# Issuing the store of the attention values from ScalarE, beside the copy that feeds it, instead of from SyncE

## The reference

```
xn  = layernorm(x)
q, k, v = xn Wq', xn Wk', xn Wv'              # 16 heads of 16
s   = softmax(causal(q k') / 4) v, heads joined, times Wo'
g   = silu( (silu(xn Wg'/127) * (xn Wu'/127)) Wd'/127 )
out = x + s * g
```

## Time and profile before

| | |
|---|---|
| median of 3 runs | 954.44 us (954.1 to 955.37) |
| the profiled execution's own time | 956.07 us |
| its span in the trace | 954.3 us |
| mean granted clock of TensorE | 0.995 of full speed |
| PE busy | 917.9 us, 96% |
| ACT busy | 584.3 us, 61% |
| POOL busy | 496.0 us, 52% |
| instructions | 22760 |

### The profile page before, as it was taken

One profiled execution on the slowest core, in us unless ns is written; L12 is line 12 of the kernel. 1 busy time (PEld: TensorE's weight loads), 2 busy tenths in 40 slices (PEclk: granted clock), 3 DMA queues, 4 the chain that ended last, 5 costly groups with the idle time before them and its releaser, 6 DMA issues.

```text
span 954.3 us, 22760 instructions
## 1 busy us (share of the span) xinstructions
PE 917.9 (96%) x9065; PEld 685.9 (72%) x9065; DVE 700.1 (73%) x950; ACT 584.3 (61%) x796; POOL 496.0 (52%) x681
## 2 busy tenths in 40 slices
PE   4999999999999999999999999999999999999994
PEld 3767767776868777686877768687686877768564
DVE  6985868787786977768687786868778686777823
ACT  5265675657576665757657575666657566575771
POOL 4253644737455473645547464474645547364552
PEclk9999999999999999999999999999999999999997
DMA  7704236344442535435353543534344353444323
GB/s 242 190 26 166 83 116 188 125 162 128 156 153 102 179 118 171 136 135 161 126 173 101 192 137 124 173 125 155 119 169 147 117 175 122 161 129 151 105 93 86
DMA packets 85468, 133.97 MB, mean 140 GB/s; under 512 B 13681, under 2 KB 35953, under 8 KB 85361
## 3 DMA queue, kind: packets, MB, share of 16 engines
q1 hardware_dynamic: 85360, 132.47, 42.0%
HBM read 53.22 MB, written 25.75 MB: 83 GB/s over the span
## 4 chain that ended last, share of the span: by engine, by line
PE 81%; issue 5%; POOL 4%; ACT 3%; DVE 3%; DMA 2%; SPq 0%; POOLq 0%; ACTq 0%; DVEq 0%
PE bank L194 44%; PE values L527 12%; PE bank L434 12%; PE bank L494 9%; PE bank L447 3%; POOL o_compact L568 2%; ACT probs L502 2%; DMA o_reciprocals<-scratch_r 1%; ACT o_hi L575 1%; DVE gated L379 1%; DVE row_max L457 1%; POOL probs L509 1%; PE bank L463 1%; PE bank L670 0%; DMA mean_and_rstd<-scratch_m 0%
## 5 line engine op out<-in xcount | busy, mean ns | idle before, releaser
L457 DVE TENSOR_REDUCE row_max<-bank 128x2 f32<-128x768 f32 (+3 forms) x352 | 384.8, 1124 | 61.6 <-PE bank L447 58.5
L502 ACT ACTIVATE probs<-bank 128x1024 f32<-128x1024 f32 x320 | 320.1, 1026 | 120.7 <-PE bank L494 119.3
L509 POOL TENSOR_SCALAR_AFFINE_SELECT probs<-probs 128x256 f32<-128x256 f32 (+1 forms) x448 | 194.2, 451 | 270.0 <-ACT probs L502 267.7
L527 PE MATMUL values<-probs,v 128*17 128x512 f32 (+3 forms) x2048 | 166.2, 436 | 4.9 <-POOL probs L509 4.8
L393 POOL TENSOR_TENSOR h_lo<-gated,h_hi 128x512 fp32r<-128x512 f32 x96 | 125.1, 1303 | 70.6 <-ACT h_hi L390 68.4
L434 PE MATMUL bank<-k_stack,q_stack 64*128 64x128 f32 (+3 forms) x1024 | 155.7, 364 | 2.7 <-DVE row_max L457 1.2
L494 PE MATMUL bank<-q_stack,k_stack 64*128 64x512 f32 (+3 forms) x1024 | 142.2, 350 | 1.3 <-DVE row_max L457 0.7
L434 PEld LDWEIGHTS bank<-k_stack,q_stack 64*128 64x128 f32 x1024 | 83.0, 185 | 69.7 <-issue 30.4
L494 PEld LDWEIGHTS bank<-q_stack,k_stack 64*128 64x128 f32 x1024 | 82.7, 185 | 39.2 <-issue 17.3
L366 DVE SCALAR_TENSOR_TENSOR gated<-gated,bank 128x512 f32<-128x512 f32 x96 | 65.8, 685 | 58.1 <-ACT gated L363 58.1
L194 PE MATMUL bank<-xt_hi,wg_hi 128*128 128x256 f32 x384 | 99.2, 292 | 2.3 <-DVE gated L379 2.3
(11 more groups left out here) (123 smaller groups left out, 1602.9 us busy)
## 6 DMA issues: line engine op xcount, KB each, us to landing
k_stack<-qk_hi SPq DMA_DIRECT2D x64, 256.0 KB, 2.5
q_stack<-qk_hi SPq DMA_DIRECT2D x64, 256.0 KB, 2.6
scratch_o<-o SPq DMA_DIRECT2D x64, 256.0 KB, 2.3
x_again<-x SPq DMA_DIRECT2D x16, 512.0 KB, 4.8
k_stack<-qk_lo SPq DMA_DIRECT2D x32, 256.0 KB, 2.5
q_stack<-qk_lo SPq DMA_DIRECT2D x32, 256.0 KB, 2.7
o_compact<-scratch_o SPq DMA_DIRECT2D x32, 256.0 KB
o_reciprocals<-scratch_r SPq DMA_DIRECT2D x32, 256.0 KB
```

What stands on the lines that cost most here:

```text
L457: signal(e.tensor_reduce(rows, scores, axis=AX.X, op=ALU.max), "d_sm")
L502: signal(e.activation(PR[:, (SCORES * beta + k) % SLOTS, :, :], both(banks), ACT.Exp, scale=SCALE_S), "d_ex")
L509: last = e.affine_select(out=diag, in_=diag, compare_op=ALU.is_ge, fill=0.0, base=0, pattern=[[0, many], [1, P]], channel_multiplier=-1)
L527: last = nc.tensor.matmul(PVB[32 * c:32 * c + VW, j * P:S], V[par][:, j, 4 * g + c, :], PR[:, (SCORES * beta + 5 * g + kind) % SLOTS, pari ...
```

## The change

SP's part of a third `pv` unit goes to ACT. The two waits (for the older readers of the scratch, `s_oc`, and for the copy, `d_ov`) and the DMA are the same, but they now stand in ACT's queue, right behind ACT's own copy.

```diff
             elif en == "act" and part == 2:
                 wait(e, s_ost, 16 * (4 * beta + g))
                 after(e, "f_pv", beta, k)
                 signal(e.activation(O[:], PVB[:], ACT.Copy), "d_ov")
-            elif en == "sp" and part == 2:
                 wait(e, s_oc[g // 2], 32 * beta)
                 after(e, "d_ov", beta, g)
                 e.dma_start(scratch_o[g * P:(g + 1) * P, :], O[:]).then_inc(s_ost, 16)
```

## The result

| | before | after |
|---|---|---|
| median | 954.27 us (4 runs, 951.81 to 955.37) | 963.43 us (4 runs, 963.04 to 964.56) |
| ratio, 95% interval | | 1.0104 (1.0086 to 1.0121) |
| the profiled execution's own time | 956.07 us | 963.23 us |
| its span | 954.3 us | 961.5 us |

The kernel is 1.0% slower. By the medians it is 9.2 us, by the two profiled executions 7.2 us. The forecast was 959.5 us, 5.1 us more than the 954.44 us of the three runs that were known then.

A forecast was written before the change was run, and what follows sets the result against it. The arrival of the reciprocals' load was taken to clock each stage. 5.4 us for its delay in 12 stages less 0.3 us in the tail made 5.1 us, from 954.44 to 959.5 us; 8-in-10 range 952.5 to 963.5 us.

The forecast's parts named there:

- What bounds the kernel: Each stage is clocked by the arrival of the reciprocals' load; later grows it equally, earlier gains at most some 0.7 us.
- ACT's time and the hole: Behind ACT's copy: 0.32 us issue, next exponential 0.46 us late, PE's 0.3 us falling into its 0.43 us wait, costing nothing.
- The rival of a dear issue: At 0.98 us per DMA issue on ACT, late exponentials outgrow PE's hole: 6 us more, 960 us; chance 0.12.
- The DMA engines: Per stage: store from ACT's queue delays the reciprocals' load, 0.65 less 0.2, so 0.45 us; 5.4 us in 12 stages.
- a relief of 0.2 us: Transposed x, issued earlier, is out of the way of the burst at 560.0 to 560.5; taken as 0.2 us a stage.
- the store in ACT's ring: Store of 256 KB shares the DMA engines with the reciprocals' load; delay bounded by 0 and 0.65 us, 0.65 taken.
- the reading by which the load is hardly held up: With packets of many pieces, the rest of the reciprocals' load moves in one go and the store delays it by nothing.
- POOL's wait: Sign: POOL's wait for the reciprocals' load in middle stages near 3.3 us in place of 2.9; below 3.0 refutes.
- ACT's pause: Sign: copies on ACT followed by about 0.4 us in which ACT does no activation.
- PE's waits for POOL's mask: Sign: PE's waits for POOL's masked probabilities ahead of `pv 1 0` near 10 us in place of 4.8.
- a new wait for ACT's probabilities: Sign of being wrong: PE shows a new large wait for ACT's probabilities.
- The tail: End of the kernel: `ob 1 0`, freed from the copy's wait, issued some 1.2 us earlier; counted as -0.3 us.

The follow-up runs named there:

- zeros_behind: Kernel before with the zeros of the q stack moved behind the load of the reciprocals in SP's list; 945.98 us, ratio 0.9908.
- xt_held: Changed kernel, but SP waits for the last copy before it issues the load of the transposed x; 955.93 us, ratio 1.0025 to the kernel before.
- zeros_behind_act: Changed kernel with the zeros of the q stack moved behind the load of the reciprocals; 952.93 us, ratio 0.9980 to the kernel before.
- xt_early: Kernel before, all stores on SP, with the load of the transposed x moved ahead of the last store, right behind the reciprocals' load; 959.57 us, ratio 1.0053.
- only_last_act: Against the kernel before, only the store of a batch's last group is issued by ACT, the other three by SP; 961.73 us, ratio 1.0079.

## Why the prediction was right and wrong

**What bounds the kernel: right.** Each stage is clocked by the arrival of the reciprocals. The load's use is 0.60 us later and the stage grows by 0.56 us. Where the load comes 2.4 us earlier in the stage (zeros_behind), the stage shrinks by 0.73 us, from 56.44 to 55.71, and no more: I had said some 0.7 us. The reading that a few engines first write the zeros and then the rest of the load is borne out too. The trace has the times at which the load's semaphore moves. In the stage at 552 four of its last eight steps come 3.1 to 3.6 us behind the issue and four at 5.2 to 6.1 us, with 3 to 4 engines at work between the two groups; in the same stage of zeros_behind all eight come at 4.5 to 5.1 us.

**ACT's time and the hole: right.** Expected were 0.32 us for the issue, 0.46 us for the exponential and 0.3 us at `gu 1 2`. Measured are 0.33, 0.54 (1.11 less 0.57 us from the copy's start to the next exponential) and 0.40 us, and xt_held shows them nearly all hidden in PE's two waits. I put nothing in the sum for them, and the load's delay accounts for the stage without them: both POOL's start and `pv 1 0` are 0.60 us later in the mean. The rival of a dear issue is out (0.33 to 0.34 us in all 64 cases). But zeros_behind_act shows that they are hidden only because PE waits there for something else.

**The DMA engines: wrong, and this is the step that failed.** I wrote that the transposed x "is worth nothing by itself" when it comes earlier, and then credited it with a relief of 0.2 us; the price was to come from the store in ACT's ring, 0.65 us. It is the other way round. The transposed x forward costs 0.46 us from issue to use without any second ring (xt_early), and the stores on ACT with the transposed x in its place cost 0.14 us (xt_held). Together that is the 0.60 us of the changed kernel, where I had 0.45; that they add up so exactly is within the spread of the means (only_last_act, which has both causes, has 6.49 us, less than xt_early). I had looked at when its reader needs it and not at who is still being served when it starts. The row was there: between 558 and 559 only 3 to 4 engines were at work, at 47 GB/s, and the transposed x moved forward fills this stretch to 295 GB/s while the last part of the reciprocals is on its way.

On the rule of the Trainium skill in "DMA: Bandwidth & Descriptors", section "Queues, rings and completion order", that an engine takes its rings in turn by whole packets: the 0.14 us agree with the reading by which the load is hardly held up, but no run shows the order of packets on one engine. In the packet records of the stage that was read above, 88 of the store's 128 packets begin by 566.5 us and nearly all the others from 567.25 us on, when SP's queue begins the last of its own; this looks as if they had stood behind these and not taken turns. The same section says that an engine takes the descriptors of a ring in order, while a later one may still finish before an earlier one. xt_early does not contradict this, and it shows that standing first in a ring does not protect a load from what stands behind it.

**The size, and luck.** The forecast of 5.1 us has the right sign and about half of the measured size. That it came as near as this is partly luck: 0.65 us for the rings less 0.2 us of relief gives 0.45 us a stage, of which the first is nearly nothing and the second has the wrong sign. For the same reason most of the signs that I had named came in although they were named for another cause: POOL's wait 3.44 us (3.3 forecast), the transposed x 3.6 us earlier, ACT's pause 0.51 us (0.4), the stage 56.99 us (56.8). They can't tell the two causes apart; only the experiments did. One sign did not come: PE's waits for POOL's mask near 10 us. They are 5.0 us, because the 0.3 to 0.4 us of ACT's lateness, which I had put into this hole myself, now stand ahead of `gu 1 2`. And PE has a new wait for ACT's probabilities, which I had called a sign of being wrong; it is 3.2 us in all, and what a stage grows by comes out without it, since it only moves PE's standing still.

Twelve stages at 0.60 us would be 7.2 us, as much as the profiled executions differ by, but this match is chance: the eleven stages between the two starts of POOL give 6.1 us and the ends the rest. The medians differ by 9.2 us. xt_early and xt_held add up to 0.78%, the change to 1.04% (0.86 to 1.21). What is left, about 2.5 us, has no cause shown. In the profiled executions it is not in the middle stages, where xt_early and the changed kernel are equally long.

**The tail: no gain seen.** Freed from the copy, `ob 1 0` is issued 3.03 us behind `or 1 0` in place of 3.82. But now it stands ahead of the store. The chain that ended last, kernel after:

```profile
931.70 0.67 ACT o L533
932.41 0.04 issue
932.45 4.13 DMA scratch_o<-o
936.60 0.61 ACT o L533
...
940.27 2.02 DMA sums<-scratch_o
```

The store takes 4.13 us to land, and the last copy waits for it. From the issue of `or 1 0` (919.85 before, 928.98 after) to `od 1 1` it is 11.31 us before and 11.29 us after: what the freed wait gave, the new one took. I had counted -0.3 us.

## What to carry to other kernels

When an issue is taken out of a queue, look at what moves forward in its place, and at which transfer is still under way then: a load that nobody needs yet can slow one that everybody waits for, even from behind it in the same queue. A wait in front of an issue was also a brake, and `xt_held` shows that it was worth more than the freed queue. A cost that falls into another wait is free only until that wait is mended, and an issue on a computing engine belongs behind the work that others wait for, not directly behind its own producer.

## What was not expected of the hardware

- A DMA of 1 KB in 128 rows of 8 bytes to HBM, 64 times in the kernel, took 4.9 us to land (median), and other stores landed late beside it (256 KB: 5.1 us in place of 2.3, and 2.7 in the changed kernel). The kernel with it was 3.2% slower. Why was not tried.
- In the stage read here a DMA issue on ACT behind its own copy stops ACT for 0.51 us: 0.08 us until the copy's end is seen (563.77 + 0.60 to 564.45), 0.33 us for the issue, 0.10 us to the next activation.
- With zeros of 64 KB into four rows in front, a load of 256 KB ends in two groups: the first four of the last eight steps of its semaphore are done after 3.7 us in the mean of twelve stages, the last four after 6.0. Without them in front all are done after 5.1 us, so that from issue to use it is 5.18 us in place of 6.05. POOL still waits for the load then (0.10 us or more in each of the twelve stages). The first four are done 1.2 us later than with the zeros in front; the load is issued 1.5 us earlier in the stage there, into other traffic, and what of the difference comes from that was not tried.
